# Value products of two key tiles issued together on TensorE, with a longer ring of exponentials

## The reference, cut to what matters

```python
scores = jnp.einsum('bqhd,bkhd->bhqk', q, k) * scale      # cross: 1601 keys
attn = jax.nn.softmax(scores, axis=-1)
out = jnp.einsum('bhqk,bkhd->bqhd', attn, v)
...
scores = jnp.where(causal, -jnp.inf, scores)              # self: 512 keys, masked
```

## Time and profile before

| | |
|---|---|
| Median of 3 runs | 3208.51 us (3202.58 to 3218.04) |
| The profiled execution, its own time | 3208.35 us |
| Its span, first to last instruction | 3206.7 us |
| TensorE (matmul) busy | 2653.5 us, 83% |
| VectorE busy | 1813.1 us, 57% |
| ScalarE busy | 1433.4 us, 45% |
| Cross-attention, first maximum to last output copy | about 305 to 1587 us |
| Self-attention, first maximum to last output copy | about 1843 to 2203 us |
| Mean granted TensorE clock | 0.907 |

### The profile page before, as it was taken

The page is one execution under the profiler, slowest core; times in us unless marked ns, Lnnn a source line. Parts: engine busy times, 40 slices in busy tenths (PEclk is TensorE's granted clock), DMA queues, the critical chain, the costliest instruction groups (busy, mean ns, idle before and its releaser), DMA issues. The chain is left out here.

```text
span 3206.7 us, 58377 instructions
## 1 busy us (share of the span) xinstructions
PE 2653.5 (83%) x14654; PEld 1345.6 (42%) x14655; DVE 1813.1 (57%) x3856; ACT 1433.4 (45%) x2927; POOL 490.1 (15%) x650
## 2 busy tenths in 40 slices
PE   7996999999999999999769689885440599999980
PEld 5663233333333333333145344442330377777750
DVE  4564887878787878788256466663231122222223
ACT  2331576767676767677623256663110122212210
POOL 2445000000000000000034511110225200000006
PEclk9997899999999999999989899997665799999995
DMA  6777554545544544553046366663435111011116
GB/s 209 216 232 146 70 74 67 68 68 66 70 64 69 69 64 69 64 69 50 22 153 203 128 140 138 144 136 104 146 122 185 61 33 33 31 31 33 33 47 186
DMA packets 524824, 313.65 MB, mean 98 GB/s; under 512 B 312112, under 2 KB 486848, under 8 KB 524480
## 3 DMA queue, kind: packets, MB, share of 16 engines
q1 hardware_dynamic: 492752, 256.93, 39.4%
q0 software_dynamic: 11392, 37.76, 3.6%
q10 hardware_dynamic: 20464, 16.40, 1.6%
HBM read 188.91 MB, written 121.26 MB: 97 GB/s over the span
## 5 line engine op out<-in xcount | busy, mean ns | idle before, releaser
L717 DVE TENSOR_REDUCE att_cross_neg_max<-att_cross_ps_s 128x1 f32<-128x401 f32 x2048 | 1031.4, 567 | 217.6 <-PE att_cross_ps_s L636 215.0
L792 ACT ACTIVATE att_cross_probs<-att_cross_ps_st 128x512 f32<-128x512 f32 (+1 forms) x1664 | 883.0, 601 | 349.0 <-PE att_cross_ps_st L655 331.0
L636 PE MATMUL att_cross_ps_s<-att_cross_k_pack,att_cross_q_pack 96*128 96x401 bf16 x2048 | 666.8, 349 | 28.8 <-DMA att_cross_q_pack<-q_parts 28.3
L655 PE MATMUL att_cross_ps_st<-att_cross_q_pack,att_cross_k_pack 99*128 99x512 bf16 (+1 forms) x1664 | 642.6, 389 | 37.0 <-issue 30.8
L670 PE MATMUL att_cross_ps_o<-att_cross_probs,att_cross_v_tiles 128*32 128x512 f32 (+1 forms) x3328 | 452.4, 616 | 1.0
L636 PEld LDWEIGHTS att_cross_ps_s<-att_cross_k_pack,att_cross_q_pack 96*128 96x128 bf16 x2048 | 203.4, 99 | 402.7 <-DVE att_cross_neg_max L717 233.4
L655 PEld LDWEIGHTS att_cross_ps_st<-att_cross_q_pack,att_cross_k_pack 99*128 99x128 bf16 (+1 forms) x1664 | 165.7, 100 | 343.7 <-ACT att_cross_probs L792 194.8
L717 DVE TENSOR_REDUCE att_self_neg_max<-att_self_ps_s 128x1 f32<-128x128 f32 (+3 forms) x512 | 223.5, 485 | 140.8 <-PE att_self_ps_s L639 137.3
L792 ACT ACTIVATE att_self_probs<-att_self_ps_st 128x256 f32<-128x256 f32 (+3 forms) x512 | 205.7, 441 | 127.7 <-PE att_self_ps_st L658 118.8
L1742 DVE COPY moe_hiddenT<-moe_ps_h 128x256 f32<-128x256 f32 x142 | 60.2, 424 | 296.9 <-PE moe_ps_h L1652 296.9
L1706 ACT ACTIVATE moe_silu<-moe_ps_g 128x352 f32<-128x352 f32 x142 | 65.8, 463 | 301.0 <-PE moe_ps_u L1644 301.0
(11 more groups left out here) (208 smaller groups left out, 2906.0 us busy)
## 6 DMA issues: line engine op xcount, KB each, us to landing
att_cross_k_pack<-k_parts SPq DMA_DIRECT2D x192, 200.1 KB, 6.6
k_parts<-in_part SPq DMA_DIRECT2D x72, 256.0 KB, 3.2
in_rows<-in_ctx_dram SPq DMA_DIRECT2D x24, 512.0 KB, 4.2
v_rows<-in_v_biased SPq DMA_DIRECT2D x24, 512.0 KB, 2.9
att_cross_q_pack<-q_parts SPq DMA_DIRECT2D x192, 64.0 KB, 7.5
att_cross_v_tiles<-v_rows SPq DMA_DIRECT2D x128, 96.0 KB
att_self_k_pack<-k_parts SPq DMA_DIRECT2D x192, 64.0 KB, 3.1
att_self_q_pack<-q_parts SPq DMA_DIRECT2D x192, 64.0 KB, 3.2
```

Source lines behind the costliest of these rows:

```text
L636: mm = nc.tensor.matmul(ps_s[bank][:, 0:w], qp[v.buf][0:SROWS, j, q * P:(q + 1) * P], kp[v.buf][0:SROWS, j, s:s + w], start=True, stop=not ...
L655: mm = nc.tensor.matmul(ps_st[bank_of_step[s]][0:rows, q0:SEQ], kp[u.buf][0:MROWS, j, t * P:t * P + rows], qp[u.buf][0:MROWS, j, q0:SEQ], ...
L717: nc.vector.tensor_reduce(nmax[v.odd][:, j * QT + q, i:i + 1], ps_s[bank][:, 0:w], AX.X, ALU.max, negate=True).then_inc(s_read, 1)
L792: nc.scalar.activation(pr[0:rows, (u.odd * STEPS + s) % RING, q0:SEQ], ps_st[bank_of_step[s]][0:rows, q0:SEQ], ACT.Exp).then_inc(exp_done, 1)
```

## The change

Two things change in `attention`. TensorE issues the products of two tiles as one group, behind every eighth score: behind step 8k + 11 those of tiles 2k and 2k + 1. The last group of a unit, behind step 3 of the next unit, has one tile in cross-attention (13 is odd) and two in self-attention. And the ring of exponentials has 13 places (cross) or 16 (self) in place of 8. No matmul, reduction, exponential or DMA is added or taken away.

```diff
--- before.py
+++ after.py
@@ -448,7 +448,7 @@
     tiles = [(t, min(P, kv - t * P)) for t in range(-(-kv // P))]
     NT = len(tiles)
     STEPS = NT * GH
-    RING = 8
+    RING = 16 if causal else 13
     LAG = 5
     BUFS = 4
     VBUFS = 4 if causal else 2
@@ -465,6 +465,7 @@
     SLOTS = NP + 1
     TAIL = 11 if causal else 15
     KT = 3 if causal else 6
+    last_tiles = range((NT - 1) // 2 * 2, NT)
     step_of = [STEPS - TAIL + (k - NP) * STEPS / NP for k in range(NP)]
     EARLY = sum(s < 0 for s in step_of)
     assert EARLY > KT and (units - 4) % 4 == 0
@@ -679,11 +680,13 @@
                         scores(u, s)
                         while todo and todo[0][0] < s + 0.5:
                             maxima(*todo.pop(0)[1:])
-                        if s % GH == GH - 1:
+                        if s % (2 * GH) == GH - 1:
                             if s >= GH:
+                                products(u, s // GH - 2)
                                 products(u, s // GH - 1)
                             elif before:
-                                products(u.next(-1), NT - 1)
+                                for t in last_tiles:
+                                    products(u.next(-1), t)
                         while todo and (todo[0][0] < s + 1 or s == STEPS - 1):
                             maxima(*todo.pop(0)[1:])
 
@@ -696,7 +699,8 @@
                         unit(Unit(i, r), 3)
                 for r in range(1, 4):
                     unit(Unit(units // 4 - 1, r), 3 - r)
-                products(Unit(units // 4 - 1, 3), NT - 1)
+                for t in last_tiles:
+                    products(Unit(units // 4 - 1, 3), t)
 
             @block.vector
             def _(dve):
```

## The result

The changed kernel takes 3243.03 us (median of 4 runs, 3241.99 to 3247.33), the kernel before 3208.28 in the runs beside it (3202.58 to 3218.04): ratio 1.0108, 95% interval 1.0081 to 1.0134. It is 1.1% slower, as forecast. The table is in us, from the profiled execution of each kernel.

The account below looks back on a forecast made before the run. PE was taken to bound cross-attention, with DVE close behind; in self-attention a unit's first score waits for the maxima's DMA. 3208.35 us + 26 (cross-attention) + 9 (self-attention) = 3243 us, range 3200 to 3275.

Parts of the forecast that it names:

- The saving: On PE, each joined pair of tiles' products saves 0.22 us; 256 pairs, 56 us if PE bounds everywhere.
- DVE's four banks: In cross-attention, four score banks cannot cover a pair's silence: DVE idles 0.72 us behind every pair, 0.94 with a score.
- The two bad places: In a cross unit, DVE idles 1.42 us where the maxima are turned and 1.20 at the start, behind ACT's output copy.
- The unit: Each undisturbed cross-attention unit loses 0.98 us; over 31 units, 30 us.
- the two walks: Both issue orders carried through a cross unit by timing rules: 36.86 us before, 37.84 after.
- Last unit: Last cross unit, no maxima, ACT bounds: eight steps take 5.2 us in place of 4.8, six times, +3 us.
- Loop boundaries: At seven hardware-loop boundaries with PE's clock low, less loss and cheaper joins give about 1 us each, 7 us back.
- Cross-attention: The whole cross-attention stage: 30 + 3 - 7 = +26 us.
- Self-attention: Transposition 0.26 us later, behind GpSimd's split: +0.26 us a unit, +0.47 where the DMA lands early; +9 us (8 to 15).
- The sum: Whole kernel: 3208.35 + 26 + 9 = 3243 us, 1.1% slower.
- The ring: The longer ring of exponentials in attention costs nothing.
- Rivals 1 and 2: Whole kernel: first, the saving comes through, 3152 or 3185 us, chance 0.11; second, a draw, 3211 or 3220, chance 0.14.

Follow-up runs that it names:

- experiment 5: Kernel before with longer ring, cross-attention maxima over 200 of 401 scores, and products in pairs in cross-attention alone: 3189.7 us, ratio 0.9968 to the kernel before.
- experiments 6 and 7: Output copy at step 9, not 5: on the changed kernel, 3224.3 us; on pairs in cross-attention alone with maxima over 200 of 401 scores, 3175.43 us.
- experiment 8: Changed kernel with the maxima of cross-attention placed four steps earlier: 3202.86 us, ratio 1.0003 to the kernel before.
- experiment 3: Kernel before with the longer ring and products in pairs in self-attention alone: 3206.34 us, ratio 1.0020 to the kernel before.
- experiment 9: Kernel before with the maxima of self-attention placed 3.5 steps earlier: 3237.57 us, ratio 1.0111 to the kernel before.
- experiment 11: Kernel before, single products, with only the maxima of cross-attention placed four steps earlier: 3192.19 us, ratio 0.9940 to the kernel before.

## Why the prediction was right, step by step

- **The saving is real** (0.22 forecast, 0.23 measured for each joined pair): right. The forecast had it from one sample, the row. What decided was what stands around it.
- **DVE's four banks** force idle time behind a pair: right. The forecast counts idle time from where the next reduction could have started, 0.09 us ahead of the end of a record, and the trace from that end. So 0.72 and 0.94 behind clean pairs stand for 0.63 and 0.85 in the trace, where 0.64 and 0.86 (0.94 in one place) were measured. Taking the load off DVE gave 1.01 us a unit back (experiment 5). The Trainium skill says in TensorEngine Tiling (Array Packing), Performance Considerations, that tiling speeds up TensorE but not the evacuation of PSUM. The trace agrees: a reduction costs 0.48 us with pairs as without. What ran out here was the number of banks between the two engines, by the idle rows, and not DVE's rate.
- **The two bad places**: right in their rows. At the turn 1.42 was forecast, 1.33 as the trace counts, and 1.34 measured; at the start of a unit 1.20, or 1.11, and 1.21 measured in a unit that follows an undisturbed one, 1.53 in one that does not. The role of ACT's output copy is shown by 0.47 us in experiments 6 and 7. The turn's place as a price is not borne out: moving the turn to another place between the pairs gave 0.11 a unit (experiment 8), where the difference of the two idle times, 1.42 - 0.94, promised 0.48.
- **The unit**: +0.98 forecast, +0.97 measured. The prediction's list of DVE's idle time before the change does not add up to its 5.9 us: 13 x 0.41 + 3 x 0.2 + 0.4 is 6.3 at the least. The trace has twelve such places in a unit, not thirteen, and the total of 5.9 is about right (36.98 - 30.9 = 6.1). The loss is the difference of the two walks and does not use the list. Where the walk was too kind to ACT is seen with DVE out of the way: 36.6 expected in experiment 5, 36.94 measured.
- **Last unit**: +3 forecast, +4.42 measured. The period of 5.2 was right: where no pair of this unit met the low clock, in experiments 5 and 8, it took 32.39, +2.77. A pair at the low clock was left out, and another one in the unit ahead.
- **Loop boundaries**: -7 forecast. Two units cost +0.65 where two undisturbed ones cost +1.94, so 1.3 came back at each; six of them lie between output copies, 7.8 in all. The size is right, as six times 1.3 and not seven times 1, but in part by luck: PE's two gaps at a boundary are 0.75 us shorter together with pairs (4.92 to 4.17 on average). The forecast had no such term. About 0.5 a boundary is left for its own two, the spared loss and the cheaper joins at the low clock.
- **Cross-attention**: +26 forecast, +25.8 measured: 16.4 + 2.6 + 4.4 + 6 x 0.65 = 27.3 from the first output copy on, and 1.6 less ahead of it. That this meets the forecast within 0.2 is luck in part: the two pairs at the low clock (+3.0) and the stretch ahead of the first output copy (-1.6, where one unit's loss of +1 was forecast; it differs by 2.8 us between kernels that issue the same work there) had no term, and they nearly cancel.
- **Self-attention**: +9 forecast. +5.5 in the profiles and about +6 by the times of experiment 3, +2.4 by the averages of four kernels with pairs there and eight without, with a spread of 7 us among those without. The mechanism was there: the transposition waits for GpSimd and comes 0.35 us later behind the first score, where 0.26 was forecast. (The wait of 0.63 is longer because tile 0's products, which stood there, are gone.) That would give 32 x 0.35 = 11 us if this loop bounded every unit. And experiment 9 showed that the loop of the earlier trace rows is not the only limit near: this term was mis-sized, and the range of 8 to 15 us given with it was missed.
- **The sum**: 3243 forecast, 3243.03 measured. That the two agree to the microsecond is luck. Self-attention gave 3.5 us less than its term, and 2.7 us came from outside the two stages. The medians of the kernel before lie 8 us apart between sets of runs (3200.79 to 3209.02).
- **The ring** at no cost: right (1.0004).
- Rivals 1 and 2 needed DVE to be deep in work when a pair begins. By its idle time behind the pairs it never has more than four banks of work then, as forecast.

Open are why the turn's place is worth so little, why the gaps at a boundary are shorter with pairs, the cause of the second "issue" gap at a boundary, why TAIL 19 takes it away, and how self-attention's waits in experiment 9 share the loss.

## What to carry to other kernels

A saving on the busiest engine is worth having only as far as the engines behind it are buffered: grouping work saves the switch (0.23 us) but lengthens the silence (1.26 to 2.13 us here), and four banks of 0.48 us are 1.8 us deep. Before joining two groups, compare the longest silence with the depth in banks times the time of one, at the places where a bank is held or a copy stands in the way, and count each bad place once per unit. And when a small reordering moves the time by much more or less than its place in a steady stretch allows, look at the loop boundaries first.

## What the runs showed of the hardware

- At each of six hardware-loop boundaries PE of the kernel before stands still twice within some 6 us, for 2.15 to 2.76 and for 2.39 to 2.67 us, with no releaser, and its granted clock falls to 0.54 to 0.66 on average over the 15 us behind the first gap (the earlier trace rows shows 0.66). With the maxima placed four steps earlier the second gap disappears at all six boundaries, and the boundary costs 3.65 us less (experiment 11). Six times 3.65 is 22 us, about as much as the change costs in all of cross-attention. What the engine fetches or waits for in these gaps, no row shows.
- Where no maxima are left, a pair of products was met by a clock near its lower level (3.1 to 3.5 us in place of 1.9) once or twice in six of seven kernels with pairs, and single groups never in six kernels. A pair does not force it: in experiment 5 no pair met it, and in experiment 8 the last unit took 32.39 us at a mean clock of 1.00, though in the unit ahead of it one pair took 3.07. Which waits make the clock fall there, no run shows.
- Four float32 matmuls of 32 columns with 512 moving elements, into four quarters of one bank, cost 0.86 us in a row with others of their kind, 0.09 more on entry and 0.14 more on the way back to full matmuls.
- The units between two loop boundaries repeat their length within 0.02 us (37.95 each time, or 36.98; the first one and the last ones of the stage differ), so an effect of 0.05 us a unit is readable from one profile, where the total needs many runs for 3 us.
